# Loads of the first tiles in rows of 4 KB, their patterns taken as not-zero, and bias products behind tile 1

## What is computed

```python
w = jnp.einsum('nd,dkio->nkio', embedding, weight)
b = jnp.einsum('nd,do->no', embedding, bias)
As = [jnp.eye(N), A, 2.0 * (A @ A) - jnp.eye(N)]
x_g = jnp.einsum('knm,bmc->bnkc', jnp.stack(As), x)
out = jnp.einsum('bnki,nkio->bno', x_g, w)
x = _layernorm(x + out + b)
```

## Time and profile before

| | us |
|---|---|
| median of 3 runs | 1244.4 |
| lowest, highest run | 1244.18, 1246.44 |
| span of the profiled execution | 1241.0 |
| PE busy in it | 1224.7 |
| DVE busy in it | 770.7 |
| ACT busy in it | 212.8 |

### The profile page before, as it was taken

The page is one execution under the profiler, slowest core; times in us unless marked ns, Lnnn a source line. Parts: engine busy times, 40 slices in busy tenths (PEclk is TensorE's granted clock), DMA queues, the critical chain, the costliest instruction groups (busy, mean ns, idle before and its releaser), DMA issues.

```text
span 1241.0 us, 16426 instructions
## 1 busy us (share of the span) xinstructions
PE 1224.7 (99%) x5880; PEld 1027.3 (83%) x5880; DVE 770.7 (62%) x1875; ACT 212.8 (17%) x388; POOL 66.7 (5%) x54
## 2 busy tenths in 40 slices
PE   7999999999999999999999999999999999999997
PEld 6888888888888887888888888888888888888877
DVE  5825898887768877788635564472246355644725
ACT  5722111120111101220111111020111111110101
POOL 0000000000000000000000010010000000100100
PEclk9999999999999999999999999999999999999999
DMA  9832112231213110101011123033001111230331
GB/s 343 336 102 61 31 47 77 61 103 36 61 56 102 52 39 22 48 22 43 15 35 35 34 69 68 17 106 82 1 26 43 35 35 34 69 68 17 85 70 37
DMA packets 142329, 81.34 MB, mean 66 GB/s; under 512 B 110096, under 2 KB 121104, under 8 KB 140432
## 3 DMA queue, kind: packets, MB, share of 16 engines
q1 hardware_dynamic: 142240, 80.19, 22.5%
HBM read 55.00 MB, written 25.17 MB: 65 GB/s over the span
## 4 chain that ended last, share of the span: by engine, by line
PE 94%; DVE 3%; DMA 1%; SPq 1%; issue 1%; ACT 0%; DVEq 0%
PE ps L727 30%; PE ps L728 30%; PE ps L831 22%; PE ps L745 8%; PE ps L766 2%; PE ps L767 2%; DMA raw<-in_at 1%; DVE ring L1103 1%; DVE nat L1103 1%; PE ps L739 1%; SPq L1149 0%; DVE sml L1043 0%; DMA ring_x<-y1d 0%; DVE sml L1034 0%; DVE nat L1038 0%
## 5 line engine op out<-in xcount | busy, mean ns | idle before, releaser
L727 PE MATMUL ps<-B,xs 128*128 128x512 f32 (+1 forms) x1680 | 656.3, 391 | 1.5 <-DVE xs L993 1.5
L728 PE MATMUL ps<-B,xs 128*128 128x512 f32 (+1 forms) x1680 | 649.4, 387 | 0.0
L727 PEld LDWEIGHTS ps<-B,xs 128*128 128x128 f32 x1680 | 315.8, 188 | 63.6 <-issue 1.6
L728 PEld LDWEIGHTS ps<-B,xs 128*128 128x128 f32 x1680 | 315.7, 188 | 61.8
L831 PE MATMUL ps<-Tw,xs 128*128 128x512 f32 x1280 | 309.0, 391 | 1.0 <-DVE ring L1103 1.0
L831 PEld LDWEIGHTS ps<-Tw,xs 128*128 128x128 f32 x1280 | 238.8, 188 | 54.3 <-DVE ring L1103 5.0
L981 DVE TENSOR_TENSOR ring<-ps,rrep 128x512 f32<-128x512 f32 (+1 forms) x95 | 64.6, 684 | 241.8 <-PE ps L728 230.7
L1103 DVE SCALAR_TENSOR_TENSOR nat<-ps,embn,nat 128x128 f32<-128x128 f32 x448 | 153.9, 344 | 43.2 <-PE ps L831 43.0
L1103 DVE SCALAR_TENSOR_TENSOR ring<-ps,embn,ring 128x128 f32<-128x128 f32 x512 | 175.7, 343 | 0.0
L745 PEld LDWEIGHTS ps<-W,ring 128*128 128x128 f32 x896 | 111.6, 191 | 7.5 <-DVE ring L981 1.9
L745 PE MATMUL ps<-W,ring 128*128 128x128 f32 x896 | 113.3, 275 | 0.7 <-DVE ring L981 0.6
(11 more groups left out here) (68 smaller groups left out, 546.4 us busy)
## 6 DMA issues: line engine op xcount, KB each, us to landing
raw<-in_at SPq DMA_DIRECT2D x13, 1024.0 KB, 16.3
td<-ring SPq DMA_DIRECT2D x32, 256.0 KB, 2.0
ring<-td SPq DMA_DIRECT2D x128, 64.0 KB, 2.6
ring<-in_xn SPq DMA_DIRECT2D x16, 256.0 KB, 2.8
ring_x<-in_xt SPq DMA_DIRECT2D x32, 128.0 KB, 3.1
ring_x<-y1d SPq DMA_DIRECT2D x32, 128.0 KB, 3.2
out<-nat SPq DMA_DIRECT2D x15, 256.0 KB, 2.4
y1d<-ring SPq DMA_DIRECT2D x14, 256.0 KB, 2.8
```

What stands on the lines that cost most here:

```text
L727: pe.matmul(bank, x[:, 0, m, :], of, start=m == 0, stop=False)
L728: mm = pe.matmul(bank, x[:, 1, m, :], of, start=False, stop=ends and m == NT - 1)
```

## The change

It touches the head alone, the first 16 tiles of `adj`.

- **Loads.** The first x part of both chunks comes from a new input `x0` in one transfer with rows of 4 KB, into `ring`. Tiles 0 and 1 follow, in halves with rows of 4 KB, then embedding and bias, and only then the diagonal, in halves in turns with those of tile 2. Tiles 3, 4 and 15 are loaded in halves too.
- **Patterns of tiles 0 and 1** are `raw != 0` (DVE, L996 of the new kernel), which needs neither the diagonal nor ACT's count. Their comparison with the diagonal, for the count alone, comes later (step `equal`, behind tile 7 and tile 10).
- **Slots.** Tiles 0 to 7 land in slots 14, 15, 8 to 13 and their patterns go to slots 0 to 7, so DVE no longer waits there for ACT. Tiles 8 to 15 are made in place as before; the load of each waits until the tile that was in its slot is counted and compared.
- **Bias products** become 8 of 32 x 128 by 32 x 128 in fp32 (two node tiles in one, with a block-diagonal bias), behind tile 1's products. The four steps of chunk 1, quarters 2 and 3, tiles 0 and 1 wait for the copies of the banks and come behind them.
- **PE starts on zeros**: DVE clears a part of `ring_g`, and PE runs 11 products of it, 128 x 128 by 128 x 512 in bf16, into a bank that is overwritten later.

```diff
-PIECES = {0: 4, 1: 2, LAST: 4}
+PIECES = {0: 4, 1: 2, 2: 2, 3: 2, 4: 2, LAST: 2}
+COUNTED = {2: 2, 3: 2, 4: 2, LAST: 2}
+SLOT = [14, 15, 8, 9, 10, 11, 12, 13] + list(range(8, NT))
+BEFORE = {SLOT[m]: m for m in range(8)}
+WARM = 11
...
+            if m == 7 or m == 10:
+                put("equal", 0, 0, 0, 0 if m == 7 else 1)
+            of = [(j, c) for c in range(NC) for j in range(2) if j == 0 or c < 2 or 2 <= m < 12]
+            for j, c in [(0, 0), (0, 1), (1, 0), (1, 1), (0, 2), (0, 3)] if m == 0 else sorted(of) if m == LAST else of:
+                put("first", j, 0, c, m)
+            if m == 1:
                 put("bias")
+                for c in (2, 3):
+                    for k in (0, 1):
+                        put("first", 1, 0, c, k)
...
+                        pe.wait_ge(s_zero, 1)
+                        for _ in range(WARM):
+                            pe.matmul(ps[:, 7, :], ring_g[:, 0:64].bitcast(BF16), ring_g[:, 0:256].bitcast(BF16),
+                                      start=True, stop=True)
+                    if s.kind == "bias" and not general:
                         pe.wait_ge(s_e, 32)
+                        for t in range(NT // 2):
+                            mm = pe.matmul(ps[:, 2 + t // 4, t % 4 * P:(t % 4 + 1) * P], embt_s[:, t * P:(t + 1) * P],
+                                           b0t, start=True, stop=True)
+                            if t % 4 == 3:
+                                mm.then_inc(s_b0, 1)
...
-                        if k == 0 and c == 3:
-                            pe.wait_ge(s_b0c, 2)
+                        if k == 0 and j == 1 and c > 1:
+                            pe.wait_ge(s_b0c, c - 1)
...
+                        if k < 2:
+                            dv.tensor_scalar(B[:, k, cols], there, 0.0, None, ALU.not_equal, ALU.bypass).then_inc(s_B, 1)
+                            continue
...
-                        dv.wait_ge(s_nz, tile_at[s])
+                        if SLOT[k] == k:
+                            dv.wait_ge(s_nz, sign_at[s._replace(kind="sign")])
...
+                sp.dma_start(ring[:, 4:6, :], x0).then_inc(s_x[0], 16)
+                for m in range(2):
+                    for i, cols in enumerate(loaded(m)):
+                        sp.dma_start(raw[:, SLOT[m], cols], at[m * P:(m + 1) * P, cols]).then_inc(s_at[m][i], 16)
...
-                    if not s_at[m]:
-                        sp.wait_ge(s_nz, tile_at[Step("tile", 0, 0, 0, m - 7)])
...
+                    if m >= 8:
+                        gone = max(BEFORE[m], m - 7) if m < LAST else BEFORE[m]
+                        sp.wait_ge(s_nz, sign_at[Step("sign", 0, 0, COUNTED.get(gone, 1) - 1, gone)])
+                        sp.wait_ge(s_B, tile_at[Step("tile", 0, 0, PIECES.get(gone, 1) - 1, gone)])
+                        if BEFORE[m] < 2:
+                            sp.wait_ge(s_eq, BEFORE[m] + 1)
```

## The result

| | before | changed |
|---|---|---|
| median, us | 1244.18 | 1238.94 |
| lowest, highest of 5 runs | 1242.47, 1246.44 | 1238.19, 1240.98 |
| span of the profiled execution | 1241.0 | 1237.0 |

The ratio is 0.9959, with the 95% interval 0.9949 to 0.997: 5.2 us faster, where 6.2 was forecast. Two more measurements of the changed kernel, under the experiments, gave 0.9957 and 0.9954.

A forecast was written before the change was run, and what follows sets the result against it. PE, busy 1224.7 of 1241.0 us, was taken as the bound, so only time ahead of tile 2's first product counts: 23.31 - 16.8 - 0.3 = 6.2 us, giving span 1234.8, median 1238.2, range 1236.6 to 1240.6.

The forecast's parts named there:

- Step 1: Program start: x comes in one load of 0.52 MB, issued first, and lands at 4.5 us, bounds 4.0 and 5.0.
- Step 2: Left half of tile 0: 0.52 MB at 340 GB/s takes 1.54 us and lands at 6.05, bounds 1.23 and 2.3 us.
- Step 3: First pattern: DVE's not-zero takes 0.5 us, bounds 0.42 and 0.69; PE's first product at 6.65 us against 10.83.
- Step 4: Tile 0 on PE: 12 products in 2.7 us, with 0.1 us of small waits, done at 9.4.
- rival (b): First products: zeros don't lift the clock, or it has fallen by the first pattern; gain 5.0 us, 1239.4, chance 0.15.
- Step 5: Tile 1 on PE: ready at 9.95 after a wait of 0.45 us, then 12 products, done at 12.7.
- Step 6: Bias products behind tile 1: 16 records in 2.0 us, now on the path, done at 14.7.
- Step 7: Bias bank copies: 0.3 us of wait, bounds 0 and 1.0, then 8 products in 1.8 us; ends at 16.8.
- Step 8: Tile 2: lands at 16.0, right half ready at 17.3 and needed at 18.6, so covered by 1.3 us.
- Step 9: Later tiles: tiles 4 and 8 are tight, tile 8 with 0.2 us of cover; 0.3 us taken, bounds 0 and 1.
- (a): First loads: rows aren't why the start is slow, 209 to 301 GB/s stay; gain 5.2 us, 1239.2, chance 0.20.
- its likeliest case: Whole program: the forecast itself, 6.2 us gained, span 1234.8 and median 1238.2, chance 0.48.

The follow-up runs named there:

- e5: Changed kernel with DVE's comparisons of tiles 2 to 7 waiting for ACT's counts again: median 1240.79 us, ratio 0.9969.
- e10: Changed kernel with 18 products of zeros in place of 11, measured a second time: median 1236.87 us, ratio 0.9941.
- e11: Changed kernel with 18 zeros and tiles 5 to 7 loaded, counted and compared in halves: median 1237.4 us, ratio 0.9942.
- e12: Changed kernel with 18 zeros, tiles 5 to 7 in halves and tile 0's left half loaded as two quarters: median 1239.6 us, ratio 0.9957.
- e6: Changed kernel with tiles 0 and 1 compared with the diagonal again, its halves loaded ahead of tile 0's: median 1240.83 us, ratio 0.9973.
- e4: Changed kernel with tiles 0 and 1 loaded in 2 KB rows, still waited for by halves: median 1239.09 us, ratio 0.9965.
- e2: Changed kernel without the 11 products of zeros: median 1239.72 us, ratio 0.9968.
- e7: Changed kernel with bias products between zeros and tile 0, their operands loaded behind the first x part: median 1238.63 us, ratio 0.9958.
- e8: Changed kernel with bias products and their operands ahead of tile 0, and 14 zeros in place of 11: median 1238.49 us, ratio 0.9955.
- e1: Changed kernel without an edit, measured again as a control: median 1238.0 us, ratio 0.9957.
- e9: Changed kernel without an edit, a control on another chip: median 1239.4 us, ratio 0.9954.
- e3: Changed kernel with 18 products of zeros in place of 11, first measurement: median 1238.17 us, ratio 0.9956.

## Why the prediction was right, and where its steps were not

The median is 1238.94, in the range and 0.7 us above the forecast. The span says more: 1237.0 against 1234.8 forecast, which is 2.2 us too low. By steps:

- **Step 1** held: x lands at 4.55 (4.5 forecast).
- **Step 2 failed.** The left half of tile 0 lands at 7.39, not 6.05, and beyond its bound (4.5 + 2.3). I took 340 GB/s from the row of the kernel before at 4 us; the changed kernel moves 217 and 238 at 4 to 6 us, with rows of 4 KB. The term of the sum is 2.8 us instead of 1.54; the half lands between 6.9 and 7.4 in all kernels that load it whole right behind x. The single microsecond that I took, since it was the same place of the program, was not that of the changed kernel. In the kernel before, too, it was the best of the first ones: 283 and 229 GB/s follow it.
- **Step 3** held: 0.42 us for 512 elements, 0.48 from landing to product. With step 2 the first product is 1.2 us late.
- **Step 4 failed** by 1.7 us, since rival (b) came true in a form near to its second one: the zeros lift the clock, but it has fallen by the fourth product, behind a gap of 2.09 us that is itself the work of step 2. I had written that the gap is about 1 us. 12 products take 4.5 us instead of 2.7. That this happens isn't sure in each execution, as e5 shows.
- **Step 5:** the wait of 0.45 for tile 1 did not come, because PE was late. **Step 6** held: 1.98 us for the 16 records. **Step 7:** no wait for the copies (0.3 forecast). Together 0.6 us given back (0.45 of step 5, and 1.94 us instead of 2.1 for step 7), so tile 2 starts at 19.11 and not 16.8: 1.2 + 1.7 - 0.6 = 2.3.
- **Step 8** held in its mechanism: no wait at tile 2. The right half lands at 17.5 and not 16.0, and is ready at 18.8 and not 17.3, 1.5 us late, about as much as step 2. e5 gives the cut of ACT's count a size: with it back in the chain, 1 to 2 us are lost.
- **Step 9:** tile 8 is ready at 40.6 and needed at 19.1 + 6 x 3.64 = 40.9, so the reserve of 0.3 was not touched. But it was to be ready at 38.4 and needed at 38.6: the loads were 2.2 us late here too, and only the late PE hid it. **Had PE kept the times of the forecast, it would have waited at tile 8**, an estimated 2 us by this trace and 0.8 by that of e10, where tile 8 is ready at 39.4. So steps 2 and 4 were not the only ones between the forecast and its 6.2 us. e11 and e12, which would reach tile 8 at 39.3 and 39.2, wait there 0.66 and 1.02. Step 9 missed tile 5, the first tile that is compared whole: the versions without slow products that leave it whole wait there 0.37 to 1.60 us.

Two of the signs that the prediction named did not come: a first product by 7.5 us (it is 7.87), and over 300 GB/s at 4 to 6 us. The 16 records of bias in 2.0 us, no wait at tile 2 and PE busy from 17 us on did.

So the gain at tile 2 is 4.2 us, and that is what the prediction put under (a) and (b) together (4.5 us, first pattern at 7.3), not its likeliest case. The forecast for the median came out close because two errors met: the span was forecast 2.2 us too low, and 3.4 us were put on it for the time outside the span, where the changed kernel has 1.9, because 1.4 of the 3.4 were the short profiled execution of the kernel before. That is luck and not insight. Against it stands that the medians show a gain of 5.0 to 5.9 us, nearer to the 6.2 than the traces; which of the two is the gain of the head stays open.

The parts by the runs: DVE freed from ACT's count about 2 us (e5; 1.1 to 1.4 by the head against the changed kernel's own traces), the not-zero patterns about 1.4 by the head and 2.2 to 2.4 by the means (e6), the 4 KB rows about 0.5 by the head and 1 by the median (e4), the 11 zeros 0 to 1.7 (e2), all of them measured by taking one away. They overlap, since each part covers a wait of another, and need not add up to the gain. The old bias products, 32 of them ahead of everything, were not put back alone, so what their move is worth by itself stays open; e7 and e8 say only that the new ones can stand on either side of tiles 0 and 1.

## What to carry to other kernels

When the start of a kernel is sped up, work out for every later tile when it is ready and when it is needed, not only for the next one: here the versions that brought PE to tile 2 by 1.4 to 2.7 us earlier than e1 and e9 gave back from under half of it (e10) to all of it (e8) as waits at tile 2, 5 or 8. Warm-up products should last until the real ones start: with 11 of them the clock fell in three traces of the changed kernel out of three, with 18 in none of four. More of them is cheap, since those behind the rise of the clock cost half, as long as they don't stand in the way of the first data (e12). For the rate of the first loads, read the single microseconds of the trace at the low end, and don't take the best one.

## What the runs showed of the hardware

- **Zeros count.** 11 products of zeros in bf16, 128 rows, go 0.43 us apart themselves and lift TensorE to 2.4 GHz for the products behind them (0.23 us per 512 columns at 8.21 to 8.68). Bias products of 16 rows in fp32, 7.08 us of them without a gap, did not the earlier trace rows. The Trainium skill, TensorE: Matmul & The Clock Gate, Part 1, has activity as what lifts the clock; the trace agrees for the zeros, and does not for those bias products, behind which the first 10 products were still slow.
- **What lowers it is not the gap alone.** Behind a gap of 1.70 us before tile 2 the level stayed high. Behind 11 zeros it fell with gaps of 1.69 (e1), 1.76 (e9), 1.90 (e4) and 2.09 us, not at once but three to five products later, and in e6, with 2.84, the products are slow from the first one. In e7, zeros and bias products, it fell with one of 1.43. In e5, with 11 zeros and the same start as e1, it stayed. (Its gap reads 1.42 where e1's reads 1.69, but the last zeros and the first product start at the same times in both; the difference is the length given to the last zero.) Behind 18 zeros it stayed, with gaps of 0.45 (e3), 0.85 (e10) and 1.06 (e11). What the engine did ahead of the gap matters too, and something that differs between executions; the runs don't say more.
- **A dip of the loads at 4 to 6 us.** 217 and 238 GB/s at 4 to 6 us, 258 and 287 in e1, with the DMA engines shown as busy, in rows of 4 KB, where 13 to 14 us has 430. Its cause is open; with 2 KB rows the first half landed no later (7.05 against 6.99).
- **Small loads go with a dip, too.** A second one, 215 GB/s at 11 us in the changed kernel and 234 and 271 at 10 to 12 in e1, is where the operand of the bias products with 32 rows lands (11.1 and 11.2). In e7, which loads it ahead of tile 0, the dip is gone from there (426 at 10 us) and 167 and 184 GB/s stand at 4 to 6 us, with tile 0 1.5 us later. But e8 has the same order and 210 and 307 there, and its tile 0 comes only 0.5 us later, so the size of the effect differs from one execution to the next. The rows of e7:

```profile
4.00:5.00 1.00, 1.00 (x4) 0.38 (x3) 0.00 (x0) 0.11 (x1) 0.00 (x0) 1.00 1.16 167
5.00:6.00 1.00, 1.00 (x7) 0.53 (x6) 0.39 (x1) 1.00 (x2) 0.00 (x0) 1.00 0.72 184
...
10.00:11.00 1.00, 1.00 (x4) 0.81 (x3) 0.59 (x3) 1.00 (x1) 0.00 (x0) 0.50 1.04 426
```
